# Prologue: Wb through ScalarE's queue, Wg and the token tiles through SyncE's, and three of four first norms on VectorE

## The chip, the core and the metric

The kernel runs on one core of a Trainium2 chip. The core has TensorE (matmuls, into the eight PSUM banks), VectorE, ScalarE, GpSimd and SyncE. Transfers between the DRAM and SBUF run on 16 DMA engines; here they are issued by SyncE (queue q1) and ScalarE (queue q10). The metric is the device time of one execution in microseconds, as a median of several.

## What is computed

Two transformer blocks in float32 on x of 32 x 128 x 512, conditioned by cond_1024 of 32 x 512. Cut to what the start of the kernel computes:

```python
def _sln(h, w, ln_g, ln_b, Wg, bg, Wb, bb):
    mu = jnp.mean(h, axis=-1, keepdims=True)
    var = jnp.mean((h - mu) ** 2, axis=-1, keepdims=True)
    ln = (h - mu) / jnp.sqrt(var + EPS) * ln_g + ln_b
    gamma = (w @ Wg.T + bg)[:, None, :]
    beta = (w @ Wb.T + bb)[:, None, :]
    return gamma * ln + beta
...
h = _sln(hidden, w, ln_g, ln_b, Wg, bg, Wb, bb)
qkv = (h @ Wqkv.T + bqkv).reshape(B, N, num_heads, hd, 3)
...
out = out @ Wp.T + bp
h1 = out + hidden
h2 = _sln(h1, w, ln_g, ln_b, Wg, bg, Wb, bb)
return h2 + h1
```

The first block is this layer (16 heads, no MLP), the second an RMS norm with a scale and shift from the condition, attention with one head, and an MLP of 512 to 2048 to 512.

## The kernel before

The work comes in 32 tiles of 128 tokens x 512 features, one for each batch item. Four tiles make a group (GB = 4); queries and keys are computed a group at a time. A float32 operand is split into a high and a low part in float32r, and a product takes three matmuls (w_hi a_hi, w_hi a_lo, w_lo a_hi). There is no scheduler: each engine runs its own hand-written list in order, and engines wait for one another by semaphores. TensorE's list runs from the prologue through stage A (first block), stage B (attention of the second) and stage C (its MLP) without a barrier, so what starts late at the head of that list ends late.

The prologue does four things. (1) **Film product**: `cond` times Wg and Wb, which lie in the tile `wgb` (index 0 and 1), arriving in three pieces (`wgb_piece`: rows 0 to 255, 256 to 383, 384 to 511, each announced by `wgb_in[k]` at 32, that is when both halves are there). TensorE takes k = 0 and 1, then transposes token tile 0 (`norm_a`), then takes k = 2 and 3. It waits before the first of these for `consts_in` at 32, which means that both `cond` and `cols` (the bias columns) have landed. ScalarE copies the result to `fv0`, TensorE transposes it (`film_t`), VectorE makes the scale and shift tables of the first group from it (`first_tables`). (2) **Norms**: VectorE takes mean and variance of each token tile in `xa` (`var_a`, `mean_var`, `add_eps`), GpSimd computes `rstd1` by a power of -0.5 and normalizes the tile in place (`norm_a` on GpSimd), and TensorE transposes it into a bank. (3) ScalarE (tiles 0 and 2) and VectorE (1 and 3) scale and shift the transposed tile out of the bank and round it to `h_hi`; VectorE makes the four `h_lo` (`norm_low`). (4) **Weights**: the key and query weights arrive in `stage_a[0]` and `stage_a[1]`; GpSimd splits the first 128 columns of the keys' into `wk_hi` and `wk_lo` (`wk_first`), ScalarE and VectorE the rest. `first_keys` is TensorE's first product: it needs all four `h_hi`, then `wk_lo`, then all four `h_lo`; the queries behind it need `wq_lo`.

`keep_warm(n)` issues n matmuls on the identity that nothing reads, into a bank that is free. `ident` and all else are there by 1.5 us. In the trace a float32 matmul is two records.

SyncE issues, in order: token tiles 0, 1, 2; Wg and Wb for each of the three pieces; token tile 3; the stages; token tiles 4 to 7, each behind a wait for the transposes of the tile that it replaces (`n_done`). ScalarE issues `cond` and `cols`.

## Time and profile before

| | us |
|---|---|
| median of 3 runs | 1483.64 |
| lowest and highest of them | 1482.88, 1484.57 |
| the profiled execution's own time | 1484.56 |
| its span | 1482.8 |

The profile is of one execution. Busy time is given for each engine; waits are inferred from the semaphores, and the chain of waits follows the last instruction back to what released it. Ends of matmuls are modelled, so for TensorE the starts are the firmer reading. The weight loads of TensorE are listed as an engine of their own (PEld).

### The profile page before, as it was taken

The numbers are of one execution on the slowest core, as the hardware profiler recorded it, in microseconds if no ns is written. First come the engines' busy times: TensorE is split into PE (matmuls) and PEld (weight loads), VectorE is DVE, ScalarE is ACT, GpSimd is POOL, SyncE is SP. The second block draws the span as 40 slices with busy tenths as digits, with TensorE's granted clock in tenths as the row PEclk, the third lists the DMA queues.
The fourth block names the chain that finished last, engine by engine and source line by source line (L and its number), as shares of the span: only waits on it lengthen the run. The fifth ranks groups of instructions, "written<-read, shape, count | busy, mean of one in ns | idle before, by whom it ended". The sixth has DMA issues, their size and how long they took to land. (4 is left out here: it accounts for less than half of the span.)

```text
span 1482.8 us, 24226 instructions
## 1 busy us (share of the span) xinstructions
PE 1470.2 (99%) x8712; PEld 1194.1 (81%) x8712; DVE 937.5 (63%) x1878; ACT 670.1 (45%) x2023; POOL 623.4 (42%) x544
## 2 busy tenths in 40 slices
PE   8999999999999999999999999999999999999999
PEld 5888888888888668878888788888888888888887
DVE  6677777777776676877766644763358434763354
ACT  4656556565553455656766433332324323332210
POOL 5756666666654556766846102401123102401001
PEclk9999999999999999999999999999999999999999
DMA  7222232222213544787554864545464554545332
GB/s 258 69 75 98 72 106 73 79 101 72 81 63 122 194 147 130 252 314 251 202 174 143 305 227 171 170 156 215 162 194 135 195 194 172 169 156 214 135 135 93
DMA packets 92792, 232.58 MB, mean 157 GB/s; under 512 B 9664, under 2 KB 17856, under 8 KB 87552
## 3 DMA queue, kind: packets, MB, share of 16 engines
q1 hardware_dynamic: 90848, 216.24, 42.5%
q10 hardware_dynamic: 1824, 14.79, 2.4%
q8 instruction: 70, 1.15, 0.3%
q14 instruction: 50, 0.41, 0.1%
HBM read 174.17 MB, written 56.82 MB: 156 GB/s over the span
## 5 line engine op out<-in xcount | busy, mean ns | idle before, releaser
L1336 ACT ACTIVATE pa<-bank,neg_max 128x128 f32<-128x128 f32 x512 | 181.8, 409 | 136.4 <-DVE neg_max L1744 136.4
L729 PE MATMUL bank<-w_hi,g_hi 128*128 128x512 f32 x512 | 200.5, 392 | 0.0
L731 PE MATMUL bank<-w_hi,g_lo 128*128 128x512 f32 x512 | 199.3, 389 | 0.0
L730 PE MATMUL bank<-w_lo,g_hi 128*128 128x512 f32 x512 | 199.3, 389 | 0.0
L1227 PE MATMUL bank<-op_hi,ring 128*128 128x512 f32 x448 | 174.9, 390 | 1.3 <-DVE u2p L2170 0.7
L1231 PE MATMUL bank<-op_hi,ring 128*128 128x512 f32 x448 | 174.3, 389 | 0.0
L1229 PE MATMUL bank<-op_lo,ring 128*128 128x512 f32 x448 | 174.3, 389 | 0.0
L2332 POOL TENSOR_TENSOR pa<-pa,rec 128x512 f32<-128x512 f32 x128 | 143.1, 1127 | 54.1 <-DVE rec L1767 53.9
L2304 POOL TENSOR_TENSOR xrc<-xrc,b 128x512 f32<-128x512 f32 x32 | 49.7, 1583 | 267.5 <-DMA xrc<-x_dram 267.5
L1597 ACT ACTIVATE sum<-sum,cols 128x512 f32<-128x512 f32 x128 | 92.0, 722 | 113.6 <-DVE sum L2170 113.5
L1336 ACT ACTIVATION_READ_ACCUMULATOR pa<-bank,neg_max 128x1 f32 x512 | 127.3, 249 | 0.0
L729 PEld LDWEIGHTS bank<-w_hi,g_hi 128*128 128x128 f32 x512 | 96.1, 188 | 20.2 <-issue 0.7
L731 PEld LDWEIGHTS bank<-w_hi,g_lo 128*128 128x128 f32 x512 | 96.1, 188 | 19.9
L730 PEld LDWEIGHTS bank<-w_lo,g_hi 128*128 128x128 f32 x512 | 96.2, 188 | 19.6
L1744 DVE TENSOR_REDUCE neg_max<-bank 128x4 f32<-128x512 f32 x128 | 83.4, 678 | 44.3 <-PE bank L813 44.3
L2448 POOL TENSOR_TENSOR rstd<-ve,neg_half 128x1 f32<-128x1 f32 x24 | 14.2, 590 | 220.9 <-DVE ve L2138 220.9
L2170 DVE TENSOR_TENSOR sum<-bank,p 128x512 f32<-128x512 f32 x32 | 22.1, 691 | 129.9 <-PE bank L1231 129.7
L2304 POOL TENSOR_TENSOR xra<-xra,bp 128x512 f32<-128x512 f32 x32 | 47.2, 1476 | 128.7 <-DMA xra<-xt_in 128.7
L1227 PEld LDWEIGHTS bank<-op_hi,ring 128*128 128x128 f32 x448 | 84.1, 188 | 20.5 <-DVE u2p L2170 1.6
L1231 PEld LDWEIGHTS bank<-op_hi,ring 128*128 128x128 f32 x448 | 84.1, 188 | 17.4
L1229 PEld LDWEIGHTS bank<-op_lo,ring 128*128 128x128 f32 x448 | 84.1, 188 | 17.4
L1762 DVE COPY pta<-bank 128x512 f32<-128x512 f32 x128 | 79.5, 682 | 28.6 <-PE bank L820 28.5
(263 smaller groups left out, 3546.6 us busy)
## 6 DMA issues: line engine op xcount, KB each, us to landing
ring<-w_dram SPq DMA_DIRECT2D x32, 1792.0 KB, 7.5
rows<-st_dram SPq DMA_DIRECT2D x32, 512.0 KB, 4.4
hid_dram<-sum SPq DMA_DIRECT2D x64, 256.0 KB, 2.2
hid<-hid_dram SPq DMA_DIRECT2D x64, 256.0 KB, 2.8
w_dram<-w_parts ACTq DMA_DIRECT2D x8, 1792.0 KB, 7.1
xa<-xt_in SPq DMA_DIRECT2D x32, 256.0 KB, 4.1
xra<-xt_in SPq DMA_DIRECT2D x32, 256.0 KB, 2.8
x_dram<-h SPq DMA_DIRECT2D x32, 256.0 KB, 2.0
```

The lines of the kernel that those rows point to most:

```text
L729: nc.tensor.matmul(dst, w_hi, a_hi, start=start, stop=False)
L730: nc.tensor.matmul(dst, w_hi, a_lo, start=False, stop=False)
L731: return nc.tensor.matmul(dst, w_lo, a_hi, start=False, stop=stop)
L1227: nc.tensor.matmul(dst[:], part[:, w, 0, c, :], op_hi[:, a, c, :], start=opens and c == 0, stop=False, skip_group_check=True)
L1229: nc.tensor.matmul(dst[:], part[:, w, 0, c, :], op_lo[:, a, c, :], start=False, stop=False, skip_group_check=True)
L1231: last = nc.tensor.matmul(dst[:], part[:, w, 1, c, :], op_hi[:, a, c, :], start=False, stop=c == 1, skip_group_check=True)
L1336: last = nc.scalar.activation(pa[:, j, m, :], scores_bank[j][:, m * P:(m + 1) * P], ACT.Exp, bias=neg_max[:, j * C + m:j * C + m + 1], acc ...
L1597: nc.scalar.activation(dst[:], dst[:], ACT.Gelu, bias=cols[:, B1_COL + f:B1_COL + f + 1])\
L1744: nc.vector.tensor_reduce(neg_max[:, j * C:(j + 1) * C], scores_bank[j][:].rearrange("p (h k) -> p h k", h=C), AX.X, ALU.max, negate=True) ...
L1762: nc.vector.tensor_copy(pta[:, j].rearrange("p m q -> p (m q)"), scores_bank[j][:]).then_inc(pt_copied, 1)
L2304: nc.gpsimd.tensor_tensor(x[:, i], x[:, i], row[:], ALU.add).then_inc(ready, 1)
L2332: nc.gpsimd.tensor_tensor(pa[:, j], pa[:, j], rec[:, j * C:(j + 1) * C].unsqueeze(2).broadcast_to([P, C, P]), ALU.mult)\
```

## The change

SyncE's queue now carries token tile 0, Wg piece 0, token tile 1, Wg pieces 1 and 2, token tiles 2 and 3, and then the stages as before. ScalarE's queue carries `cond`, the three pieces of Wb, and then `cols`. VectorE normalizes token tiles 1, 2 and 3 of the first group itself (`norm_first`); GpSimd normalizes tile 0 and only computes `rstd1` for the other three. `norm_first(n)` stands behind the statistics of tile n, for tile 3 behind `first_tables`. TensorE's `keep_warm` matmuls are 3 instead of 6 ahead of the film product, one more stands between the transposes of tiles 1 and 2, and 3 instead of 2 stand ahead of `first_keys`.

```diff
@@ -450,12 +450,12 @@
                 wait(sp, bxn, b - 1)
                 sp.dma_start(xb_first[:, b % 2], tokens(x1_dram, b)).then_inc(bx_in[b % 2], 16)
 
-            for t in range(3):
-                load_x(t)
             for k in range(3):
+                if k < 2:
+                    load_x(k)
                 piece = wgb_piece(k)
-                for i, w in enumerate((wg_t, wb_t)):
-                    sp.dma_start(wgb[:, i, piece], weight(w[piece.start * P:piece.stop * P, :])).then_inc(wgb_in[k], 16)
+                sp.dma_start(wgb[:, 0, piece], weight(wg_t[piece.start * P:piece.stop * P, :])).then_inc(wgb_in[k], 16)
+            load_x(2)
             load_x(3)
             units = [wqkv[:, D:2 * D], wqkv[:, 0:D], wqkv[:, 2 * D:3 * D], wp0]
             for i in range(2):
@@ -745,7 +745,7 @@
                 last.then_inc(n_done, 1)
 
             pe.wait_ge(consts_made, 3)
-            keep_warm(6)
+            keep_warm(3)
             pe.wait_ge(consts_in, 32)
             for k in range(C):
                 if k != 1:
@@ -762,10 +762,11 @@
                                            ident[0:2 * NB, 0:2 * NB])
             last.then_inc(film_t, 1)
             norm_a(1, kp_bank)
+            keep_warm(1)
             norm_a(2, o_bank)
             keep_warm(1)
             norm_a(3, x_bank)
-            keep_warm(2)
+            keep_warm(3)
             def table_rows():
 
                 pe.wait_ge(st_made, 2)
@@ -1283,6 +1284,9 @@
         def _(act):
 
             nc.scalar.dma_start(cond[:], cond_t.rearrange("(k p) b -> p k b", p=P)).then_inc(consts_in, 16)
+            for k in range(3):
+                piece = wgb_piece(k)
+                nc.scalar.dma_start(wgb[:, 1, piece], weight(wb_t[piece.start * P:piece.stop * P, :])).then_inc(wgb_in[k], 16)
             nc.scalar.dma_start(cols[:], cols_d).then_inc(consts_in, 16)
             act.wait_ge(film_done, 1)
             nc.scalar.activation(fv0[0:2 * NB, :], ps_s[0][0:2 * NB, :], ACT.Identity).then_inc(film_copied, 1)
@@ -1672,7 +1676,15 @@
                 nc.vector.tensor_scalar(ve1[:, n % 2:n % 2 + 1], mv1[:, n % 2, 1:2], EPS_LN, None, ALU.add)\
                     .then_inc(var_ready, 1)
 
+            def norm_first(n):
+
+                dve.wait_ge(rstd_ready, n + 1)
+                nc.vector.tensor_scalar(xa[:, n], xa[:, n], mv1[:, n % 2, 0:1], rstd1[:, n % 2:n % 2 + 1], ALU.subtract,
+                                        ALU.mult).then_inc(xn_ready, 1)
+
             for n in range(GB):
+                if n > 1:
+                    norm_first(n - 1)
                 var_a(n)
                 mean_var(n)
                 add_eps(n)
@@ -1704,6 +1716,7 @@
                     .then_inc(st_made, 1)
 
             first_tables()
+            norm_first(GB - 1)
 
             wa_dst = [wk_lo, wq_lo, wv_lo, wp_lo]
             wa_src = [wk_hi, wq_hi, wv_hi, wp_hi]
@@ -2287,8 +2300,11 @@
                 nc.gpsimd.tensor_scalar(xa[:, n % GB], xa[:, n % GB], mv1[:, i, 0:1], rstd1[:, i:i + 1], ALU.subtract,
                                         ALU.mult).then_inc(xn_ready, 1)
 
-            for n in range(GB):
-                norm_a(n)
+            norm_a(0)
+            for n in range(1, GB):
+                pool.wait_ge(var_ready, 2 * n + 2)
+                nc.gpsimd.tensor_tensor(rstd1[:, n % 2:n % 2 + 1], ve1[:, n % 2:n % 2 + 1], neg_half[:, 0:1], ALU.pow)\
+                    .then_inc(rstd_ready, 1)
             first = slice(0, P)
             pool.wait_ge(stage_in[0], 16)
             nc.gpsimd.tensor_copy(wk_hi[:, :, first], stage_a[:, 0, :, first]).then_inc(wk_first, 1)
```

On TensorE, from the start of its list to the first keys (L737 is `keep_warm`, L754 the film product, L761 the transposes of its result, L744 a token tile's transposes, L849 and L850 the first keys), before:

```order
L737 MATMUL bank<-ident 128x512 x6
L754 MATMUL bank<-wgb,cond 32x512 x4
L744 MATMUL bank<-ident,xa 128x128 x4
L754 MATMUL bank<-wgb,cond 32x512 x4
L761 MATMUL bank<-ident,fv_116 128x64 x4
L744 MATMUL bank<-ident,xa 128x128 x8
L737 MATMUL bank<-ident 128x512
L744 MATMUL bank<-ident,xa 128x128 x4
L737 MATMUL bank<-ident 128x512 x2
L849 MATMUL bank<-h_hi_94,wk_hi 128x512 x4
```

and of the change:

```order
L737 MATMUL bank<-ident 128x512 x3
L754 MATMUL bank<-wgb,cond 32x512 x4
L744 MATMUL bank<-ident,xa 128x128 x4
L754 MATMUL bank<-wgb,cond 32x512 x4
L761 MATMUL bank<-ident,fv_116 128x64 x4
L744 MATMUL bank<-ident,xa 128x128 x4
L737 MATMUL bank<-ident 128x512
L744 MATMUL bank<-ident,xa 128x128 x4
L737 MATMUL bank<-ident 128x512
L744 MATMUL bank<-ident,xa 128x128 x4
L737 MATMUL bank<-ident 128x512 x3
L850 MATMUL bank<-h_hi_94,wk_hi 128x512 x4
```

Three idle matmuls have left the front, and two have come in behind the film product.

On VectorE, from the statistics of tile 3 (BN_STATS) over the tables (the five TENSOR_TENSOR on `cols`, of which the first and the last stand here) to the first low part, before:

```order
L1663 BN_STATS stats<-xa 128x6
L1668 BN_AGGR mv_62<-stats 128x2
L1672 TENSOR_SCALAR ve_63<-mv_62 128x1
L1689 TENSOR_TENSOR tmp_a<-bank,cols 128x4x4
...
L1693 TENSOR_TENSOR st_ln<-tmp_a,tmp_b 128x4x4
L1725 TENSOR_SCALAR hf<-bank,st_ln 128x128 x4
L1730 CAST h_hi_94<-hf 128x4x128
```

and of the change, from the norm of tile 2:

```order
L1682 TENSOR_SCALAR xa<-xa,mv_62,rstd_64 128x512
L1667 BN_STATS stats<-xa 128x6
L1672 BN_AGGR mv_62<-stats 128x2
L1676 TENSOR_SCALAR ve_63<-mv_62 128x1
L1701 TENSOR_TENSOR tmp_a<-bank,cols 128x4x4
...
L1705 TENSOR_TENSOR st_ln<-tmp_a,tmp_b 128x4x4
L1682 TENSOR_SCALAR xa<-xa,mv_62,rstd_64 128x512
L1738 TENSOR_SCALAR hf<-bank,st_ln 128x128 x4
L1743 CAST h_hi_94<-hf 128x4x128
```

A norm of 128 x 512 now stands ahead of the statistics of tile 3, and another between the tables and the scaling of tile 1.

On ScalarE, at the head of its list, in the changed kernel:

```order
L1286 DMA cond<-cond_t_in 128x4x32
L1289 DMA wgb<-wb_t_in 128x2x512
L1289 DMA wgb<-wb_t_in 128x512 x2
L1290 DMA cols<-cols_d_in 128x76
```

`cols` was the second transfer of this queue and is the fifth now.

## Rows read from the trace of the kernel before

**Rows 1.** The page: busy time and share of TensorE, and the chain of waits

```profile
PE 1470.2 (99%) x8712; PEld 1194.1 (81%) x8712; DVE 937.5 (63%) x1878; ACT 670.1 (45%) x2023; POOL 623.4 (42%) x544
...
PE 44%; DVE 0%; issue 0%
```

**Rows 2.** The waits of TensorE in the whole span: in total, times, longest

```profile
PE bank L849 <- DVE h_hi L1730: 1.7, 1, 1.7
...
PE bank L744 <- POOL xa L2287: 0.7, 2, 0.5
```

**Rows 3.** Timeline of TensorE's matmuls: start us, us, line, op, count, [idle before <-releaser]

```profile
9.65 1.91 PE L754 MATMUL bank<-wgb,cond 128*32 128x512 f32 x8 [0.38 <-DMA wgb<-wb_t_in]
...
15.07 1.09 PE L744 MATMUL bank<-ident,xa 128*128 128x128 f32 x8
...
16.86 0.60 PE L744 MATMUL bank<-ident,xa 128*128 128x128 f32 x4
17.30 1.88 PE L737 MATMUL bank<-ident 128*128 128x512 f32 x4
20.83 1.17 PE L849 MATMUL bank<-h_hi,wk_hi 128*128 128x512 f32 x4 [1.66 <-DVE h_hi L1730]
```

**Rows 4.** DMA traffic by windows, us: last the granted clock, DMA share, GB/s

```profile
0.00:5.00 5.00, 3.45 (x4) 1.51 (x5) 1.14 (x4) 1.28 (x1) 0.90 (x9) 1.00 0.70 199
5.00:8.00 3.00, 3.00 (x7) 1.40 (x6) 1.21 (x4) 0.00 (x0) 2.89 (x3) 1.00 0.93 324
8.00:14.00 6.00, 5.61 (x23) 1.46 (x22) 1.77 (x6) 0.00 (x0) 4.85 (x5) 1.00 1.05 402
```

**Rows 5.** DMA issues of 5.2 to 5.9 us; of 0.5 to 6.5; SyncE's issue of stages

```profile
stage_a<-wqkv_in SPq DMA_DIRECT2D x1, 1024.0 KB, 9.8
...
cols<-cols_d_in ACTq DMA_DIRECT2D x1, 38.0 KB, 3.6
...
5.52 1.37 SPq L462 DMA_DIRECT2D stage_a<-wqkv_in  x2
```

The first two rows end with the time to landing in us; the third begins with its start and its length.

**Rows 6.** DMA queues between 2.5 and 2.9 us: packets, MB, share

```profile
q1 hardware_dynamic: 61, 0.12, 77.7%
q10 hardware_dynamic: 43, 0.01, 8.7%
```

**Rows 7.** Timeline of VectorE, columns as in rows 3

```profile
12.82 0.69 DVE L1663 BATCH_NORM_STATS2 stats<-xa 128x6 f32<-128x512 f32 x1 [4.00 <-DMA xa<-xt_in]
...
15.17 0.17 DVE L1689 TENSOR_TENSOR tmp_a<-bank,cols 128x16 f32<-128x16 f32 x1 [1.26 <-PE bank L761]
...
16.11 1.37 DVE L1725 TENSOR_SCALAR hf<-bank,st_ln 128x128 f32<-128x128 f32 x4
17.51 1.44 DVE L1730 CAST h_hi<-hf 128x512 fp32r<-128x512 f32 x1
18.87 1.35 DVE L1725 TENSOR_SCALAR pa<-bank,st_ln 128x128 f32<-128x128 f32 x4
20.26 0.43 DVE L1730 CAST h_hi<-pa 128x512 fp32r<-128x512 f32 x1
...
28.08 0.74 DVE L1755 TENSOR_SCALAR qa<-bank,cols 128x512 f32<-128x512 f32 x1
```

**Rows 8.** Timeline of GpSimd, columns as in rows 3

```profile
14.00 0.56 POOL L2284 TENSOR_TENSOR rstd<-ve,neg_half 128x1 f32<-128x1 f32 x1 [0.94 <-DVE ve L1672]
14.66 2.08 POOL L2287 TENSOR_SCALAR xa<-xa,mv,rstd 128x512 f32<-128x512 f32 x1
16.69 0.61 POOL L2294 CAST wk_hi<-stage_a 128x512 fp32r<-128x512 f32 x1
17.39 1.28 POOL L2296 TENSOR_TENSOR wk_lo<-stage_a,wk_hi 128x512 fp32r<-128x512 f32 x1
```

**Rows 9.** Timeline of the weight loads of `keep_warm`, columns as in rows 3

```profile
5.13 0.34 PEld L737 LDWEIGHTS bank<-ident 128*128 128x128 f32 x1 [0.52 <-issue]
...
6.54 0.19 PEld L737 LDWEIGHTS bank<-ident 128*128 128x128 f32 x1 [0.24 <-issue]
```

## Prediction

> **What bounds the kernel now.** First the page: TensorE is busy 99% of the span, and the chain of waits is TensorE's own almost to the last instruction [rows 1]. Its waits by releaser, longest first, name single waits of the prologue [rows 2]. So nothing behind the prologue has room for this change to fill or to open, and the whole question is when TensorE gets to its first keys, at 20.83 us, and how the parts behind them follow. A microsecond there is a microsecond at the end. Then the timeline of the prologue, engine by engine, to see which chain arrives last.
>
> Of the 20.83 us the film product waits for data until 9.65, runs on to about 14, and its transposed result, through ScalarE and TensorE again, releases the tables at 15.17 [rows 3, 7]. They end when the scaling begins, at 16.11; VectorE then scales and rounds tiles 1 and 3 until 20.69 (20.26 + 0.43), which releases the first keys [rows 3, 7]. The chain that ends last is therefore: data of the film product, film product, tables, VectorE's two tiles.
>
> **Part 1, the transfers.** What the film product waits for is data. The rates [rows 4], added up, say that 1.00 MB had moved by 5 us, 1.97 by 8 and 4.38 by 14 (0.402 a microsecond). A token tile is 0.262 MB (256 KB), Wg and Wb 2.10 MB, a stage 1.05, `cond` and `cols` 0.10. Token tile 3 is complete after 3.25 MB, which had moved at 11.2 us, and landed at 12.82, where VectorE had waited 4 us for it [rows 7]; stage 0 is complete after 4.30 MB, moved at 13.8, landed at 5.52 + 9.8 = 15.3 [rows 5]. A transfer thus lands 1.5 to 1.6 us after its last bytes' turn. The first Wb piece, 1.94 MB, turn at 7.9, fits the start at 9.65.
>
> In the changed kernel TensorE's first wait is still for `cols`, which landed 3.6 us after its issue [rows 5], the second of its queue, long before it was needed. Now it stands behind all of Wb. ScalarE's queue has 0.07 + 1.05 + 0.04 = 1.15 MB up to `cols`. Between 2.5 and 2.9 us, with both queues full, they moved 61 and 43 packets [rows 6], so I take them as sharing evenly, and `cols` is complete when 2.3 MB have moved in all. At the rates of before that is at 8.9 us, landing at 10.5; at the later 402 GB/s from 5 us on (a queue never short of issued work) it is at 8.2, landing at 9.8. I take 10.1: the film product starts **0.45 us later**, not earlier, although 0.26 MB less stands ahead of its weights. The bounds are 9.3 and 10.9. Its second half needs all of Wg, complete at 2.73 MB, landing by 11.6, and TensorE comes to it at 12.5: hidden.
>
> The 324 GB/s between 5 and 8 us, at a DMA share of 0.93 against 1.05 later [rows 4], are all that a second issuer can win, at most 3 us x (402 - 324) GB/s, 0.23 MB or 0.6 us. The Trainium skill, page "DMA: Bandwidth & Descriptors", section "Issuing engines are not separate DMA queues", says that issuing from several engines saves only the issuer's time because the same 16 engines do the work; by it the landing would be the 10.5 and the sum 0.4 us worse.
>
> Tile 2 moves behind the weights: complete at 2.99 MB, landing between 11.5 and 12.2. From its arrival VectorE and GpSimd need 1.18 us to the start of the power (12.82 to 14.00, on tile 3), 0.66 from there to the norm (14.66), about 0.5 for the norm and 1.15 for the statistics of tile 3 [rows 7, 8]: tables not before 15.0 to 15.7. The film chain frees them at 15.17 + 0.45 = 15.6. The two arrive together; I count 0.45.
>
> **Part 2, the norms.** Tiles 1 and 2 were normalized by 13.06, where GpSimd's 0.94 us of idle time begin [rows 8], and needed from 15.07 [rows 3]: taking them from GpSimd gives nothing. Tile 3's norm ended at 16.74 and its transposes began at 16.86, with most of a 0.7 us wait [rows 2, 3, 8], but VectorE came to the result only at 18.87 [rows 7]. So nothing is freed there either. What is added is one norm of 128 x 512 on VectorE's chain. No row shows it: the nearest are the rounding of the same size from SBUF, 0.43 us, and the TENSOR_SCALAR of that size from PSUM, 0.74 [rows 7]. The first reads the same memory, so I take 0.45.
>
> Then an effect between engines. The rounding of tile 1 took 1.44 us and that of tile 3 0.43 [rows 7]; the slow one ended 0.28 us after GpSimd's `wk_lo` (17.39 + 1.28 = 18.67) [rows 8]. It was held by GpSimd, for 1.0 us. The Trainium skill, page "SBUF — State Buffer", section "SBUF: two separate sides", says the same: the port pair that the two share is a lock held for a whole instruction. In the change GpSimd is free when stage 0 lands (15.3, or 14.7 at the faster rate): `wk_hi` and `wk_lo` run from there for 2.0 us, until 16.7 to 17.3. VectorE's norm of tile 3 wants to begin at 16.5, and is held until 17.0 to 17.3 at worst. So the 1.0 us on the rounding goes and up to 0.8 comes back one instruction earlier. VectorE's sum: + 0.45 (film) + 0.45 (norm) - 1.0 + 0.5 (held again) = **+0.4 us**.
>
> **Part 3, the idle matmuls.** Two `keep_warm` matmuls (four records) take 1.88 us with the last one's end, 0.43 a record at the pace of [rows 9], so 0.86 for one; a tile's transposes 0.44 (16.86 to 17.30) [rows 3]. TensorE's own chain from the film transposes on is then tile 1, one idle matmul, tile 2, one, tile 3, three: 3 x 0.44 + 5 x 0.86 = 5.6 us after 15.07 + 0.45, first keys at 21.1. Before, this chain ended at 19.2 with 1.66 us of idle time behind it [rows 3]; now it ends with VectorE's, 20.69 + 0.4. Two added matmuls have used up the cover: had VectorE gained more, these would eat it. ScalarE's part (tiles 0 and 2) moves by the tables' 0.45. Behind the first keys, `h_lo`, `wq_lo`, `wk_lo` and the norm of tile 4 hang on the same VectorE list and move alike. **Sum: +0.4 us.** The profiled execution took 1484.56, its span 1482.8, the median 1483.64; added to the median this gives **1484.0**.
>
> **Rivals.**
> *Film early.* `cols` lands at 9.3 (ScalarE's queue gets more than half) and stage 0 at 14.7, so that the norm of tile 3 is hardly held. Tables then start when tile 2 allows, at 15.0, 0.2 earlier; VectorE's chain is -0.2 + 0.45 - 1.0 + 0.3, and TensorE's idle matmuls set -0.4. That gives 1483.2. For it speaks that ScalarE's 43 packets of [rows 6] were small ones, which leaves open how large ones share. Nothing gives the 3 us that would count: the arrival of tile 2 stands in the way.
> *The clock falls, slower.* At the start the weight loads of `keep_warm` come 0.86 us apart at 5.13 (0.34 busy and 0.52 idle) and 0.43 at 6.54 [rows 9], which are the half and the full pace, 1.2 and 2.4 GHz, though the granted-clock column reads 1.00 throughout [rows 4]; the engine had worked without a break since its first matmul at about 1.5. In the change three matmuls, six records, end near 6.7, just when the pace has risen, and the engine then idles until about 10.1. Before, its longest idle time behind the rise is 1.7 us [rows 2], so no row shows what 3.4 us do. If the pace falls, the first half of the film product (1.9 us [rows 3]) takes 3.6: +1.7 on the path, of which 0.4 comes back because GpSimd is done before VectorE: 1484.0 + 1.3 to 1.7, **1485.5**. If the second half and the transposes are slow too, 1487.3; the result counts as slower from 3 us on, that is only in the second form. The Trainium skill, page "TensorE: Matmul & The Clock Gate", section "Why this matters for your kernels", warns that idle gaps between bursts of matmuls let the clock fall back to 1.2 GHz; by it this rival would be the forecast, at 1485.5.
> *`cols` far behind.* If ScalarE's queue is served only when SyncE's first tiles and weights are through (3.25 MB, 11.2 us), `cols` lands at 12.8 and the start moves by 3.1: 1486.8 and beyond. Against it: [rows 6].
> *The change does not do what it says.* The three norms leave GpSimd, but on a path that they were not on; this is in the sum already.
>
> **How the numbers follow.** Forecast 0.50, own range 1483.2 to 1484.9 (the bounds of the landing, of the norm and of the hold, and half a microsecond of spread of the runs); film early 0.15; clock falls in the first half 0.25, in both 0.04; `cols` far behind 0.04; anything else 0.02. The range reaches to the first three: 1482.8 to 1486.0. A measurement of this kernel can tell about 0.2% (3 us) from no change. Within it are the first three cases: 0.91; slower 0.07; faster 0.02.
>
> **What would show it.** In the changed profile: film product at 10.1 with `cols` landing last (right), at 9.3 or 12.8 (the rivals); its eight records in 1.9 us or in 3.6; tables at 15.6; norms on VectorE of about 0.45 us, that of tile 3 longer by what `wk_lo` overlaps; the rounding of tile 1 at 0.43; no idle time between the last idle matmul and the first keys; first keys at 21.2 or just under. The prediction is wrong if the first keys start more than a microsecond off that, or if the shift at 20 us is not the shift at the end.

## The result and the profile after

The changed kernel takes **1487.57 us** as the median of 8 executions (1486.34 to 1490.09), the kernel before 1483.45 in 8 beside them (1482.71 to 1484.57). The ratio is 1.0027, with a 95% interval of 1.0017 to 1.0037: slower by 4.1 us, and beyond the forecast range of 1482.8 to 1486.0. The profiled execution took 1488.63, its span 1486.8. Two of nine later executions of the changed kernel took 1632.94 and 2869.11 us and are left out below, and one of 32 of the kernel before beside them, with 1487.43 us at a mean clock of 0.949, is kept in.

The page of the changed kernel, for comparison with [rows 1]: busy time, and the chain of waits.

```profile
PE 1471.0 (99%) x8710; PEld 1193.9 (80%) x8710; DVE 936.6 (63%) x1881; ACT 670.2 (45%) x2023; POOL 618.1 (42%) x541
...
PE 44%; DVE 0%; issue 0%
```

TensorE still does the same work in 99% of the span, and the chain is still its own. What is new stands in its waits (in total, times, longest):

```profile
PE bank L754 <- DMA cols<-cols_d_in: 4.6, 1, 4.6
...
PE bank L1228 <- DVE u2p L2183: 1.5, 1, 1.5
```

The wait of 1.66 us for VectorE ahead of the first keys [rows 2] has gone; in its place TensorE waits 4.6 us for `cols` ahead of the film product. The timeline of TensorE (start, length, line, operation), to be laid beside [rows 3]:

```profile
1.55 4.49 PE L737 MATMUL bank<-ident 128*128 128x512 f32 x6 [1.55 <-POOL ident L2283]
10.65 3.63 PE L754 MATMUL bank<-wgb,cond 128*32 128x512 f32 x8 [4.61 <-DMA cols<-cols_d_in]
14.21 1.09 PE L744 MATMUL bank<-ident,xa 128*128 128x128 f32 x4
15.23 1.91 PE L754 MATMUL bank<-wgb,cond 128*32 128x512 f32 x8
17.83 0.46 PE L761 MATMUL bank<-ident,fv 64*128 64x64 f32 x4 [0.69 <-ACT fv L1292]
...
21.31 2.74 PE L737 MATMUL bank<-ident 128*128 128x512 f32 x6
23.63 1.34 PE L850 MATMUL bank<-h_hi,wk_hi 128*128 128x512 f32 x4
```

Three lines of the timeline of before that belong beside them (tile 0's transposes, the film product's second half, the transposes of its result):

```profile
11.49 0.66 PE L744 MATMUL bank<-ident,xa 128*128 128x128 f32 x4
12.08 1.91 PE L754 MATMUL bank<-wgb,cond 128*32 128x512 f32 x8
14.68 0.46 PE L761 MATMUL bank<-ident,fv 64*128 64x64 f32 x4 [0.69 <-ACT fv L1288]
```

The film product starts 1.0 us later than before (10.65 against 9.65). Its first half takes 3.63 us instead of 1.91, tile 0's transposes 1.09 instead of 0.66, the second half 1.91 as before. The transposes of its result stand at 17.83 against 14.68 in the timeline of before, 3.15 later, and the first keys at 23.63 against 20.83, 2.8 later. The windows say why; the last three columns are granted clock, DMA share and GB/s, as in [rows 4]:

```profile
0.00:5.00 5.00, 3.45 (x4) 1.51 (x5) 1.03 (x3) 1.28 (x1) 1.03 (x9) 1.00 0.69 208
5.00:8.00 3.00, 1.04 (x3) 0.19 (x1) 0.43 (x1) 0.00 (x0) 2.38 (x2) 1.00 1.02 384
8.00:9.00 1.00, 0.00 (x0) 0.00 (x0) 0.60 (x3) 0.00 (x0) 0.25 (x1) 0.66 1.06 409
9.00:15.00 6.00, 4.35 (x12) 1.27 (x12) 3.06 (x8) 0.00 (x0) 1.67 (x4) 0.50 1.06 405
15.00:16.00 1.00, 1.00 (x6) 0.26 (x6) 0.00 (x0) 0.00 (x0) 0.92 (x2) 0.93 0.82 315
```

TensorE stops at 6.04 us, with the last of three idle matmuls. Between 8 and 9 us, while it has nothing to do, the granted clock leaves 1.00, from 9 to 15 it is 0.50, which is 1.2 GHz, and in the microsecond behind 15 it is 0.93 and so mostly back. The film product waited for `cols`, and its first half then ran at half pace.

Why `cols` lands at 10.65 is seen in the two queues (packets, MB, share), from 0 to 5 us, from 6 to 9, and from 9 to 10.25:

```profile
q1 hardware_dynamic: 408, 0.78, 49.1%
q10 hardware_dynamic: 621, 0.26, 19.4%
...
q1 hardware_dynamic: 335, 0.62, 53.6%
q10 hardware_dynamic: 333, 0.60, 51.9%
...
q1 hardware_dynamic: 241, 0.43, 90.0%
q10 hardware_dynamic: 156, 0.05, 16.4%
```

With large packets on both, from 6 to 9 us, the two queues do share evenly. But ScalarE's (q10) has a quarter of the bytes up to 5 us, since its first 528 packets, up to 3.5 us, move only 0.06 MB, the size of `cond`. (From 5 to 6 us it makes up some, with 0.25 MB against 0.09.) And its last 0.05 MB, about the size of `cols`, take 156 packets of about 0.3 KB each (1.8 from 6 to 9 us) and 1.2 us more, the last six of them after 10.0.

VectorE and GpSimd, beside [rows 7] and [rows 8]:

```profile
18.32 0.17 DVE L1701 TENSOR_TENSOR tmp_a<-bank,cols 128x16 f32<-128x16 f32 x1 [4.20 <-PE bank L761]
...
19.13 0.54 DVE L1682 TENSOR_SCALAR xa<-xa,mv,rstd 128x512 f32<-128x512 f32 x1
...
20.98 0.43 DVE L1743 CAST h_hi<-hf 128x512 fp32r<-128x512 f32 x1
```

```profile
14.71 0.61 POOL L2310 CAST wk_hi<-stage_a 128x512 fp32r<-128x512 f32 x1
15.40 1.27 POOL L2312 TENSOR_TENSOR wk_lo<-stage_a,wk_hi 128x512 fp32r<-128x512 f32 x1
```

The norm on VectorE takes 0.54 us, the rounding of tile 1 takes 0.43 instead of 1.44: GpSimd had finished at 16.67 (15.40 + 1.27), before the tables had begun. In this kernel the two no longer meet, because the film product is so late.

### The profile page after: what moved, and what is told of

Same layout as the page of the kernel before. It is cut to its first block and busy times, and to the rows that moved or that the text cites. A ratio compares the mean times of both kernels' runs of the same rounds, so it can differ in the third digit from the quotient of the medians.

```text
span 1486.8 us, 24222 instructions
## 1 busy us (share of the span) xinstructions
PE 1471.0 (99%) x8710; PEld 1193.9 (80%) x8710; DVE 936.6 (63%) x1881; ACT 670.2 (45%) x2023; POOL 618.1 (42%) x541
```

## Experiments

Theory: **the clock**. Three idle matmuls end at 6 us, TensorE then waits for `cols` until 10.7, the clock falls in the meantime, and the film product, which is on the path, runs at half pace. Rivals: the late `cols` alone, VectorE's added norms, the two idle matmuls added behind.

In what follows "mean clock" is the granted clock of a whole execution as it is listed with each, to three digits. It was 1.00 in every execution of the kernel before that was timed beside these kernels but the one named above, and 0.997 to 0.999 in all 8 of the changed kernel, so it tells for each timed execution, not only the profiled one, whether the clock fell.

| kernel | ratio to before, 95% interval | executions at 1.00, median | below 1.00, median |
|---|---|---|---|
| changed | 1.0027 (1.0017 to 1.0037) | 0 | 8, 1487.57 |
| changed, again | 1.0026 (1.0016 to 1.0036) | 0 | 7, 1488.35 |
| `warm6` | 1.0013 (1.0004 to 1.0021) | 7, 1484.77 | 4, 1487.51 |
| `cols_early` | 1.0010 (1.0001 to 1.0019) | 4, 1484.55 | 7, 1486.50 |
| `both` | 1.0003 (0.9994 to 1.0012) | 11, 1484.87 | 0 |
| `warm8` | 1.0007 (0.9999 to 1.0016) | 11, 1485.62 | 0 |
| `b_warm3` | 1.0017 (1.0009 to 1.0026) | 3, 1485.26 | 8, 1486.80 |
| `b_warm0` | 1.0020 (1.0012 to 1.0029) | 0 | 11, 1487.33 |
| `b_queues` | 1.0019 (1.0010 to 1.0027) | 7, 1485.77 | 4, 1488.88 |
| `b_queues_cols` | 1.0002 (0.9993 to 1.0011) | 11, 1484.61 | 0 |
| `b_norms` | 1.0006 (0.9998 to 1.0015) | 11, 1485.33 | 0 |
| `b_tail` | 0.9994 (0.9985 to 1.0004) | 11, 1483.90 | 0 |
| `third_way` | 0.9998 (0.9989 to 1.0007) | 11, 1483.96 | 0 |

The kernel before had a median of 1484.13 beside `warm6`, `cols_early`, `both` and `b_warm3`, of 1484.30 beside `b_norms`, `b_queues`, `warm8` and the changed kernel again, and of 1484.20 beside `b_warm0`, `b_queues_cols`, `b_tail` and `third_way`. Names with b_ are edits of the kernel before.

### The changed kernel with one part mended

`warm6`: six idle matmuls at the front again.

```diff
             pe.wait_ge(consts_made, 3)
-            keep_warm(3)
+            keep_warm(6)
```

> The changed kernel with six idle matmuls at the front instead of three; cols is still last in ScalarE's queue. Clock theory (the idle time before the film product let the clock fall): the film product starts at 10.7 us as in the changed kernel, because cols lands there, but its first eight records take 1.9 us and not 3.6; granted clock 1.00 throughout; first keys near 21.5; 0.5 to 1.2 us above before, so about 3 us below the changed kernel. Rival (the whole loss is the late cols and VectorE's added norms, the clock is a by-product): it stays 3 us or more above before.

Median 1485.36, 1.2 above before instead of 4.1. The eleven executions fall in two sets: seven at a mean clock of 1.00, 0.6 above before, four below it, 2.7 more. The profile is of one of the four:

```profile
11.53 2.72 PE L754 MATMUL bank<-wgb,cond 128*32 128x512 f32 x8 [2.53 <-DMA cols<-cols_d_in]
```

Six idle matmuls end at 9 us, and the 2.5 us that are left until `cols` are enough for the clock to fall in some executions. In this one it falls only about a microsecond after the film product has begun (granted clock 0.75 from 12 to 13 us, 0.50 from 13 on), so the first half takes 2.72 us and not 3.63. The expectation that it would stay at 1.00 was wrong; that six matmuls take away most of the loss was right.

`cols_early`: `cols` issued behind `cond`, ahead of Wb; three idle matmuls stay.

```diff
             nc.scalar.dma_start(cond[:], ...).then_inc(consts_in, 16)
+            nc.scalar.dma_start(cols[:], cols_d).then_inc(consts_in, 16)
             for k in range(3):
...
-            nc.scalar.dma_start(cols[:], cols_d).then_inc(consts_in, 16)
```

> The changed kernel with cols issued right behind cond, ahead of Wb, and three idle matmuls still at the front. Film product then waits for the first pieces of Wg and Wb only, near 7.6 us. Clock theory: the idle time ahead of it is 1.5 us, about as long as one that the kernel before survived (1.66 us), the clock stays at 1.00, first keys at 20.5, total 0 to 0.5 us below before. Rival (the clock falls after any idle time of this kind): first half of the film product 3.6 us, total 1.5 us above before. Rival (the norms on VectorE cost the time): total about 2 us above before.

Median 1486.24, 2.1 above before. The wait for `cols` is gone, and one for the first piece of Wb stands there, for the film product starts at 9.58 and not at 7.6:

```profile
9.58 2.83 PE L754 MATMUL bank<-wgb,cond 128*32 128x512 f32 x8 [2.54 <-DMA wgb<-wb_t_in]
```

My landing time was 2 us too early: on ScalarE's queue that piece landed 7.7 us after its issue. Up to 5 us that queue had moved 668 packets with 0.10 MB, and `cond` and `cols` together are 0.10 MB:

```profile
q10 hardware_dynamic: 668, 0.10, 11.9%
```

So in front of Wb these small packets hold Wb back: in the changed kernel, with `cols` last, the piece landed 6.0 us after its issue. With 2.5 us of idle time the clock fell in seven executions of eleven. The expected gain over before did not come either: the four executions at 1.00 are 0.4 above.

`both`: the two edits together.

> The changed kernel with cols issued right behind cond and six idle matmuls at the front. Clock theory: no idle time before the film product, which starts when the sixth idle matmul ends, near 9.3 us; clock 1.00; tables near 15; first keys near 20.6; total within 0.5 us of before. Rival (norms on VectorE): total still 2 us above.

All eleven executions at 1.00, median 1484.87, 0.7 above before, an interval that holds 1 and ends at 1.0012, or 1.8 us. So the norms, which this kernel has, are not the cause of the 4.1. The profile shows the first keys at 21.85 and not at the 20.6 expected; what makes them late is in the next section but one.

`warm8`: eight idle matmuls, `cols` as late as in the change.

```diff
-            keep_warm(3)
+            keep_warm(8)
```

> The changed kernel with eight idle matmuls at the front instead of three, so that they last until cols lands (10.7 us). Clock theory: no idle time before the film product, mean clock 1.00 in every execution, total 0.5 to 1.2 us above before, spread as small as that of before. Rival (the clock falls by chance whatever stands ahead): executions at 0.999 and 0.998 remain, and with them medians 2 us above or more.

No execution below 1.00. The eight idle matmuls end at 10.3 us and so delay nothing. `cols` lands as late as ever, and the film product runs at full pace:

```profile
10.97 1.91 PE L754 MATMUL bank<-wgb,cond 128*32 128x512 f32 x8 [0.62 <-DMA cols<-cols_d_in]
```

Median 1485.62 against 1488.35 of the changed kernel beside it: **2.7 us of the loss are the clock**, and 1.3 are the rest. In the profiles the first keys are 1.8 to 2.0 us sooner than in the changed kernel (21.80 against 23.61 to 23.84); the difference between that and 2.7 is of the size of the scatter discussed at the end of this section.

The changed kernel again, beside it:

> The changed kernel itself, unaltered, beside the three others on the same chip. All theories: 3 to 4.5 us above before. Clock theory: every execution has a mean clock below 1.00, and those with the lower clock take longer, 1 to 1.5 us for each step of 0.001.

Seven executions between 1487.42 and 1489.08, all below 1.00; those at 0.999 have a median of 1487.55, those at 0.998 of 1488.47. In `b_warm3` the third digit orders nothing (1485.88 and 1487.08 at 0.997), so all that is read from it here is whether it is 1.00 or below.

### The kernel before with one part of the change

`b_warm3` and `b_warm0`: three idle matmuls at the front, and none.

```diff
             pe.wait_ge(consts_made, 3)
-            keep_warm(6)
+            keep_warm(3)
```

> The kernel before with three idle matmuls at the front instead of six and nothing else changed. Clock theory: TensorE idles from 6 to 9.65 us, the granted clock goes to 0.50, the film product's first half takes 3.6 us, its transposes begin near 16.8 instead of 14.7; of these 2.1 us about 1 comes back because VectorE's rounding is no longer held by GpSimd: total 1.0 to 2.1 us above before. Rival (late cols and norms are the cause): no change.

> The kernel before without any idle matmul at the front, so that the film product starts at the half pace in every execution; all else as before. Clock theory: the first half takes 3.6 us, tile 0's transposes 1.0, and the second half 3.6 or less, depending on when the pace rises; film transposes 2.2 to 4 us later than 14.7; of this about 1 us comes back on VectorE (its rounding is not held any more) as far as ScalarE's two tiles allow: total 2 to 3.5 us above before. Rival (the film product has slack, its pace does not matter): within 0.5 us of before.

Three matmuls alone cost 2.4 us (1486.51 against 1484.13), a little more than expected. Eight of eleven executions are below 1.00. The other three are 1.1 above before in the median; that is unexplained, and three are few. The profiled one is among the three that are not, with 2.67 us of idle time ahead of the film product and its first half in 1.91:

```profile
1.55 5.49 PE L737 MATMUL bank<-ident 128*128 128x512 f32 x6 [1.55 <-POOL ident L2270]
9.71 1.91 PE L754 MATMUL bank<-wgb,cond 128*32 128x512 f32 x8 [2.67 <-DMA wgb<-wb_t_in]
```

So about the same idle time sometimes drops the clock and sometimes does not. The same three idle matmuls end at 7.04 us here and at 5.84 to 6.17 in the four profiles of the changed kernel: the pace rises at a different time from one execution to the next, and with it the idle time left changes. What decides the fall has not been found.

Without any, all executions are below 1.00, 3.1 above before. The film product's first half takes as long as in the changed kernel, though this time the clock had never risen:

```profile
9.17 3.63 PE L754 MATMUL bank<-wgb,cond 128*32 128x512 f32 x8 [9.17 <-DMA wgb<-wb_t_in]
...
22.91 1.26 PE L849 MATMUL bank<-h_hi,wk_hi 128*128 128x512 f32 x4 [2.09 <-ACT h_hi L1314]
```

The transposes of its result stand at 16.32, only 1.6 later than before (2.2 to 4 were expected). Two things add to that. A table instruction of VectorE takes 0.98 us beside GpSimd's `wk_lo` (16.90 to 18.17), of which more under `b_norms`:

```profile
17.24 0.98 DVE L1691 TENSOR_TENSOR st_ln<-tmp_a,cols 128x16 f32<-128x16 f32 x1
```

And behind the 2.09 us of idle time ahead of the first keys the clock falls once more, a microsecond after they have begun, so that most of the first keys and the first queries run at half pace (window of 24 to 26 us). This fall is also what puts the mean clock of this kernel below 1.00, since the granted-clock column does not show the slow start:

```profile
24.00:26.00 2.00, 2.00 (x6) 1.57 (x5) 2.00 (x5) 2.00 (x2) 0.00 (x0) 0.50 0.72 205
```

`b_queues` and `b_queues_cols`: the new queues on the kernel before, with `cols` behind Wb, as the change has it, and ahead of it.

```diff
-            for t in range(3):
-                load_x(t)
             for k in range(3):
+                if k < 2:
+                    load_x(k)
                 piece = wgb_piece(k)
-                for i, w in enumerate((wg_t, wb_t)):
-                    sp.dma_start(wgb[:, i, piece], weight(w[...])).then_inc(wgb_in[k], 16)
+                sp.dma_start(wgb[:, 0, piece], weight(wg_t[...])).then_inc(wgb_in[k], 16)
+            load_x(2)
             load_x(3)
...
             nc.scalar.dma_start(cond[:], ...).then_inc(consts_in, 16)
+            for k in range(3):
+                piece = wgb_piece(k)
+                nc.scalar.dma_start(wgb[:, 1, piece], weight(wb_t[...])).then_inc(wgb_in[k], 16)
             nc.scalar.dma_start(cols[:], cols_d).then_inc(consts_in, 16)
```

In `b_queues_cols` the three lines for Wb stand behind the one for `cols`.

> The kernel before with the new queues alone (Wb and then cols on ScalarE's); norms on GpSimd, six idle matmuls at the front. Late-cols theory: the film product starts at 10.7 us instead of 9.65; with TensorE idle for 1.5 us or more ahead of it the clock falls in some executions and not in others. Executions at a mean clock of 1.00: 0.3 to 1.0 us above before (part of the 1.0 comes back because VectorE's rounding is held for less); at 0.999 or 0.998: 2 to 3 us above. Rival (queues are harmless): no execution below 1.00 and no change.

> The kernel before with Wb on ScalarE's queue, but behind cond and cols, and the new order on SyncE's; norms on GpSimd, six idle matmuls. If the place of cols and the clock were all that is wrong with the queues: film product at 9.6 us, mean clock 1.00 in every execution, total as before. Theory with the port: token tile 2 lands near 11.5 instead of before 7.7, GpSimd's norms and with them wk_lo end about 1 us later than before, and hold VectorE's rounding of tile 1 for that longer: total 0.5 to 1 us above before.

With `cols` last, 2.7 us above before (1486.99 against 1484.30), 1.5 in the seven executions at 1.00 (0.3 to 1.0 were expected) and 4.6 in the four below: six idle matmuls do not reach 10.9 us. The profile is of one of the four, and the clock falls twice in it: behind the wait for `cols`, and behind a second one ahead of the first keys, for which ScalarE is late because a table instruction of VectorE took 1.22 us beside GpSimd's `wk_lo` (18.32 to 19.59). TensorE, VectorE, and the window of 26 to 28 us:

```profile
10.88 2.65 PE L754 MATMUL bank<-wgb,cond 128*32 128x512 f32 x8 [2.17 <-DMA cols<-cols_d_in]
...
24.33 1.17 PE L849 MATMUL bank<-h_hi,wk_hi 128*128 128x512 f32 x4 [2.33 <-ACT h_hi L1317]
```

```profile
18.41 1.22 DVE L1694 TENSOR_TENSOR st_ln<-tmp_a,cols 128x16 f32<-128x16 f32 x1
```

```profile
26.00:28.00 2.00, 2.00 (x6) 1.35 (x5) 1.97 (x5) 1.46 (x2) 0.00 (x0) 0.50 0.22 80
```

With `cols` early, 0.4 above, an interval around 1, never below 1.00, and the film product starts 0.35 sooner than before (9.30, with 0.78 us of waiting). The place of one transfer of 38 KB is the difference. The port theory of the expectation missed: the rounding of tile 1 takes 0.43 us there, not held at all. Token tile 2 does come later with these queues, and TensorE waits 1.30 us for GpSimd's norm of tile 3, but the first keys stand at 20.83 as before.

`b_norms`: the norms of tiles 1 to 3 on VectorE, as in the change.

> The kernel before with the norms of tiles 1 to 3 on VectorE alone; queues and idle matmuls as before. Port theory: GpSimd is free when stage 0 lands at 15.3 us, its wk_hi and wk_lo then run until 17.3 and hold VectorE's table instructions with two inputs from SBUF (one of 0.18 us should take about 1.2), which ScalarE waits for too; clock 1.00; first keys near 21.8, total about 1 us above before. Rival (the norm costs only its own 0.55 us, since the rounding of tile 1 is no longer held): total at or below before, first keys at 20.8 or sooner. Second rival (the norms carry most of the 4 us): total 3 us above.

Median 1485.33, 1.0 above before; the interval just holds 1, so the timing alone does not show a loss. The profile shows a mechanism of that size. VectorE, then GpSimd:

```profile
16.06 1.14 DVE L1701 TENSOR_TENSOR st_ln<-tmp_a,tmp_b 128x16 f32<-128x16 f32 x1
17.11 0.54 DVE L1678 TENSOR_SCALAR xa<-xa,mv,rstd 128x512 f32<-128x512 f32 x1
...
18.96 0.43 DVE L1739 CAST h_hi<-hf 128x512 fp32r<-128x512 f32 x1
```

```profile
15.85 1.31 POOL L2308 TENSOR_TENSOR wk_lo<-stage_a,wk_hi 128x512 fp32r<-128x512 f32 x1
```

The last table instruction, 16 elements a partition and 0.18 us before (L1693), takes 1.14 and ends when `wk_lo` does (17.16). It reads two operands in SBUF. ScalarE waits for it as well, and the first keys start at 21.61. The same in `both`, where it takes 1.24 us from 16.20 beside GpSimd's `wk_lo` of 16.14 to 17.41 (the kernel before, then `both`):

```profile
15.89 0.18 DVE L1693 TENSOR_TENSOR st_ln<-tmp_a,tmp_b 128x16 f32<-128x16 f32 x1
```

```profile
16.20 1.24 DVE L1705 TENSOR_TENSOR st_ln<-tmp_a,tmp_b 128x16 f32<-128x16 f32 x1
```

The Trainium skill, page "SBUF — State Buffer", section "SBUF: two separate sides", says that whichever of the two starts first gets the shared port pair for its whole instruction, and counts VectorE instructions with two SBUF inputs among those concerned, against a GpSimd instruction that reads SBUF; the trace agrees, with 1.14 and 1.24 us for an instruction of 0.18 that began 0.21 and 0.06 us after `wk_lo`. In `b_warm0` and `b_queues`, which have no norm on VectorE, a table instruction was held as well: what counts is that the tables fall into `wk_lo`'s time.

`b_tail`: the idle matmuls behind the film product as in the change.

```diff
             norm_a(1, kp_bank)
+            keep_warm(1)
             norm_a(2, o_bank)
             keep_warm(1)
             norm_a(3, x_bank)
-            keep_warm(2)
+            keep_warm(3)
```

> The kernel before with the idle matmuls behind the film product as in the change: one between the transposes of tiles 1 and 2, three instead of two ahead of the first keys. By the 1.66 us of idle time that stood there, two more matmuls of 0.86 us use it up: first keys at 20.9 to 21.0 against 20.83, total within 0.3 us of before. Rival (they are on the path with their whole length): 1.7 us above.

Median 1483.90, 0.3 below before, within the noise. The two matmuls fit into idle time that was there, as the prediction had it: no idle time is left ahead of the first keys, which start at 20.39 in the profile.

### A third kernel, and where the rest of the shift is

The runs point to small gains from the kernel before: leave queues and idle matmuls alone, let VectorE normalize only tile 3, in its idle time ahead of the tables, and keep GpSimd off the port until the tables are made.

```diff
+            dve.wait_ge(rstd_ready, GB)
+            nc.vector.tensor_scalar(xa[:, GB - 1], xa[:, GB - 1], mv1[:, 1, 0:1], rstd1[:, 1:2], ALU.subtract,
+                                    ALU.mult).then_inc(xn_ready, 1)
             dve.wait_ge(film_t, 1)
...
-            for n in range(GB):
+            for n in range(GB - 1):
                 norm_a(n)
+            pool.wait_ge(var_ready, 2 * GB)
+            nc.gpsimd.tensor_tensor(rstd1[:, 1:2], ve1[:, 1:2], neg_half[:, 0:1], ALU.pow).then_inc(rstd_ready, 1)
+            pool.wait_ge(st_made, 1)
```

> The kernel before with two edits that the runs so far point to: VectorE normalizes tile 3 alone, in its idle time ahead of the tables, and GpSimd splits the first keys' weights only once the tables are made. Port theory: the rounding of tile 1 is held until about 18.1 instead of 18.7, no table instruction is held; first keys at 20.4 (then ScalarE's tile 2 sets it, 20.3), total 0.3 to 0.5 us below before, less than the timing can tell. Rival (wk_lo or another part becomes late): first keys at 20.8 or later.

```profile
17.57 0.87 DVE L1733 CAST h_hi<-hf 128x512 fp32r<-128x512 f32 x1
...
20.54 1.16 PE L849 MATMUL bank<-h_hi,wk_hi 128*128 128x512 f32 x4 [1.30 <-ACT h_hi L1314]
```

The rounding takes 0.87 instead of 1.44, and ScalarE's tile 2 sets the first keys, at 20.54. But the second profile of the kernel before, below, has a rounding of 0.85 and first keys at 20.35 without any edit, so this is no gain shown:

```profile
17.39 0.85 DVE L1730 CAST h_hi<-hf 128x512 fp32r<-128x512 f32 x1
```

Median 1483.96 against 1484.20: nothing that the timing can tell.

The medians of the changed kernel and of before differ by 4.1 us, the first keys of the first two profiles by 2.8. Four more profiles were taken for the rest.

> The changed kernel unaltered, for its profile. Theory that the prologue carries it all: first keys at 23.5 to 25, the more the longer the clock stays down, and from there to the wait at 643 us 621 to 624 us as in all kernels so far. Rival (something later is slower in this kernel): first keys at 23.6 and more than 623 us from there.

> The same as the run before it, another execution: first keys at 23.5 to 25 and 621 to 624 us behind them by the prologue theory; 23.6 and over 623 us by the rival.

> The same again, a third execution of the changed kernel: first keys at 23.5 to 25 and 621 to 624 us behind them by the prologue theory; 23.6 and over 623 us by the rival.

> The kernel before unaltered, for a second profile of it: first keys between 20.3 and 20.9, depending on when the last pieces of Wg and Wb land; 621 to 624 us from there to the wait at 643.

Start of the first keys, and of TensorE's first waiting transpose in the second block (L1101, L1100 before), in the changed kernel (the third of the three profiles) and in the kernel before (second profile):

```profile
23.61 1.34 PE L850 MATMUL bank<-h_hi,wk_hi 128*128 128x512 f32 x4
...
645.17 0.33 PE L1101 MATMUL bank<-ident,pb 128*128 128x128 f32 x1 [0.87 <-ACT pb L1533]
```

```profile
20.35 1.16 PE L849 MATMUL bank<-h_hi,wk_hi 128*128 128x512 f32 x4 [1.29 <-ACT h_hi L1314]
...
641.69 0.33 PE L1100 MATMUL bank<-ident,pb 128*128 128x128 f32 x1 [0.85 <-ACT pb L1529]
```

The four profiles of the changed kernel have their first keys at 23.63, 23.84, 23.81 and 23.61, the two of before at 20.83 and 20.35: 3.1 us apart in the mean. From there to that transpose it is 622.5, 622.0, 621.5 and 621.6 us in the changed kernel, 622.0 and 621.3 before. From it to the end of the span it is 839.8 to 840.7 us against 839.6 and 840.0. So nothing behind the prologue is shown to be slower in it. The about 1 us between 3.1 and 4.1 is no more than the scatter of the intervals behind the prologue: 620.9 to 623.8 us up to that transpose and 839.4 to 841.6 behind it, over all kernels of this study. A part of the second scatter has a name. TensorE waits once, behind 820 us, for `u2p`, which VectorE makes, for 1.2 to 1.6 us in seven of the 17 profiles and for 0.3 to 0.7 in the others, and the seven take 0.9 us more in the mean from the transpose to the end. Two of the four profiles of the changed kernel have the long wait and neither of the two of before. That the changed kernel has it more often is not shown.

## Why the prediction was wrong

**The bound and what carries over: right.** The chain is TensorE's. The shift is 3.1 us at the first keys and 3.3 at 643 us, in the mean of the profiles.

**The clock: the step that failed.** The mechanism, its place and its price for the film product were written down as a rival (first half 3.6 us; it took 3.63), at a chance of 0.29. The forecast took the case without it, and so put the term of the clock at nothing, on the ground that no row showed what 3.4 us of idle time do. But the rows did show that the pace had risen only at the very end of what three idle matmuls last, and nothing in the trace spoke for the clock to hold through a gap twice the longest one seen. A gap of that length was a step of the change's own path, and had to be weighed as the likeliest case. What the runs showed in its place: the gap was 4.6 to 5.2 us, the clock fell in every execution, and that costs 2.7 us (`warm8`). The Trainium skill, page "TensorE: Matmul & The Clock Gate", section "Why this matters for your kernels", advises against idle gaps between bursts of matmuls, because the clock falls back in them. These runs agree: 18 of the 18 executions of the changed kernel that are counted here have a mean clock below 1.00.

**Start of the film product: right in kind, too small.** It was forecast to be later, by 0.45 us, because `cols` stands behind Wb. It was 1.0 (10.65), and in the mean of the profiles 1.3 (10.89 against 9.59); the bounds were 9.3 and 10.9, and two of four profiles lie beyond the upper. The gain in bytes came: 384 GB/s between 5 and 8 us instead of 324. It does not come from the second issuer as such, though: with `cols` early on the same two queues the rate there is 307 to 328 GB/s, as before. Even sharing was right for large packets (0.60 and 0.62 MB from 6 to 9 us). What the step left out is what small packets do: `cond`'s kept ScalarE's queue at a quarter of the bytes up to 5 us, and `cols` itself took 1.2 us behind Wb. And `cols` landed 0.4 to 0.65 us after its last packets (10.65 against 10.0 to 10.25), not 1.6: that time behind the last bytes' turn, taken from bytes added up, does not hold for it.

**The clock rival's sum was low too**, 1485.5 against 1487.6. It made the first keys 1.7 us later; they were 2.8. The start was 0.55 more than its 0.45, and tile 0's transposes took 0.43 longer at half pace, which it had at nothing. VectorE's gain was as forecast: its two tiles were done 5.51 us behind the film transposes instead of 6.01. But ScalarE's tile 2 was not (5.66 against 20.33 - 14.68 = 5.65), and TensorE's list of idle matmuls lasted 5.80, so the first keys won 0.35 only:

```profile
22.91 0.43 DVE L1743 CAST h_hi<-pa 128x512 fp32r<-128x512 f32 x1
```

```profile
22.86 0.63 ACT L1318 ACTIVATE h_hi<-pa 128x512 fp32r<-128x512 f32 x1
```

From tile 1's transposes (18.22) on, that list took 5.4 us, as the 5.6 that were forecast; so the idle matmuls had used up the cover, as forecast. The hold of 1.0 us that was to go is itself a number of one execution: in the second profile of before the rounding took 0.85, ScalarE set the first keys, and they stood 5.79 behind the film transposes, so against it nothing was won. With the clock up (`warm8`) the change costs 1.3 us and not 0.4, for these same reasons. That the rival's second form (second half and transposes slow too) gave 1487.3, close to the 1487.6, is luck: the second half took 1.91.

**The norm: 0.54 us against 0.45** taken and 0.43 to 0.74 as its bounds.

**The port: right as a mechanism, wrong in its victim.** The forecast let `wk_lo` hold the norm of tile 3. In `both` and `b_norms` it holds the table instruction ahead of that, for 1.0 us, and through it ScalarE too, which a held norm would not have delayed. That fits the 1.0 us (interval -0.3 to 2.2) that the norms on VectorE cost by themselves, where the same forecast would have made it about 0. In the changed kernel itself the film product is too late for the two to meet.

**The idle matmuls behind, and taking norms from GpSimd: right.** `b_tail` costs nothing; no tile's norm was on the path.

The parts by themselves, in executions at full clock: queues 1.5 (`b_queues`), norms 1.0, idle matmuls behind -0.3. They do not add up to the 1.3 of `warm8`, whose profile has no hold by the port: `wk_lo` ends at 16.99 and the last table instruction takes 0.19 us from 17.21. The clock adds 2.7.

## What to carry to other kernels

Idle matmuls that keep TensorE's clock up ahead of a first product must last until the data lands or nearly so (waits up to 0.8 us did no harm), not until the pace has risen; when transfers are moved, work out the new landing first and then their number. Look for what the first consumer waits on besides the bulk: a transfer of 38 KB issued behind 1 MB on the same queue lands behind the last of it, and later still if it is made of small packets. An engine that is freed earlier starts its next work earlier: ask which instructions of a neighbour on the same port it will then run beside, and whether those release more engines than the ones it used to hold.

## What the runs showed of the hardware

- The clock falls in some executions and not in others at middling idle times: with waits of 2.2 to 2.7 us ahead of the film product in the profiles, in 4, 4, 7 and 8 executions of 11 (`b_queues`, `warm6`, `cols_early`, `b_warm3`); with waits up to 0.8 us in none of 66; with 4.6 to 5.2 in 18 of 18. Waits of 1.3 to 1.7 us ahead of the first keys (the kernel before, `b_norms`, `third_way`) went with a mean clock of 1.00 in all executions but the one named under the result; those of 2.09 and 2.33 there, in the profiles of `b_warm0` and `b_queues`, dropped the clock. The kernels of the first group have two sets of times, 1.5 to 3.1 us apart, and the mean clock of an execution tells which one it is in.
- Behind a wait of 2.1 to 2.5 us the clock fell only when TensorE was at work again: 0.8 to 1.3 us after the film product or the first keys had begun (`warm6`, `cols_early`, `b_queues`, `b_warm0`). Behind 4.6 us it fell during the wait.
- Two DMA queues with large packets moved the same bytes (0.62 and 0.60 MB in 3 us). One that starts with small packets moved 0.10 to 0.26 MB up to 5 us, beside 0.78 to 0.93 of the other.
- The granted-clock column is 1.00 at the start of every profile, also where matmuls run at half pace (0.86 us apart, [rows 9]; film product of `b_warm0` in 3.63 us). It shows a fall, but not that the clock has not yet risen.
- An instruction of VectorE of 16 elements a partition can take 1.24 us beside one GpSimd instruction, when it has two inputs in SBUF.
